# ScalarE copies the turned maxima, and probability tiles and narrow value products are regrouped, in an attention and expert layer

## What is computed

```python
qkv = layernorm(x) @ Wqkv                     # q: 32 heads x 16, k: 16, v: 16
scores = einsum('bqhd,bkd->bhqk', q, k) * scale
scores = where(causal, scores + slopes * (pos_k - pos_q), -1e30)
attn = einsum('bhqk,bkd->bqhd', softmax(scores), v)
x = x + attn @ Wo
y = layernorm(x)
x = x + y @ W_base.T + b_base + expert_delta(y)   # top 2 of 8, rank 16
```

## Time and profile before

| | us |
|---|---|
| median of 3 runs | 700.57 (700.55 to 702.18) |
| the profiled execution | 700.96 |
| its span, first to last instruction | 699.2 |
| TensorE busy in it | 669.7 |
| VectorE busy | 557.4 |
| ScalarE busy | 358.6 |
| GpSimd busy | 216.9 |

### The profile page before, as it was taken

How to read it: one execution, slowest core, us unless ns; L and a number is a source line. 1 busy time by engine, 2 the same in 40 slices (tenths; PEclk the granted TensorE clock), 3 DMA queues, 4 the chain that set the end, 5 groups by cost and what they waited for, 6 DMA issues and landing times.

```text
span 699.2 us, 13261 instructions
## 1 busy us (share of the span) xinstructions
PE 669.7 (96%) x4304; PEld 305.5 (44%) x4304; DVE 557.4 (80%) x1801; ACT 358.6 (51%) x511; POOL 216.9 (31%) x366
## 2 busy tenths in 40 slices
PE   3889999999999999999999999999999999999997
PEld 2434344544344444444443343433433455555553
DVE  5899889887989889898988989899881365666565
ACT  2324647567556676666666666767667411111111
POOL 0035424233332515243352231422432412222220
PEclk9999999999999999999999999999999999999999
DMA  8578108080411443080144744225200189700001
GB/s 253 130 145 137 64 2 136 30 147 28 166 54 51 60 89 108 11 131 34 41 63 94 102 81 77 49 49 94 48 18 33 52 130 170 162 30 30 31 30 60
DMA packets 42951, 56.32 MB, mean 81 GB/s; under 512 B 6648, under 2 KB 26232, under 8 KB 42752
## 3 DMA queue, kind: packets, MB, share of 16 engines
q1 hardware_dynamic: 40296, 51.27, 37.3%
q10 hardware_dynamic: 2592, 4.26, 1.8%
HBM read 35.72 MB, written 19.79 MB: 79 GB/s over the span
## 4 chain that ended last, share of the span: by engine, by line
PE 83%; DVE 10%; DMA 3%; ACT 2%; issue 1%; SPq 1%; POOL 0%; DVEq 0%; ACTq 0%; POOLq 0%
PE psum L780 20%; PE psum L732 18%; PE psum L762 13%; PE psum L808 8%; PE psum L830 7%; PE psum L678 7%; PE psum L759 5%; DVE psum L1145 3%; PE psum L825 2%; PE psum L840 2%; ACT work L965 2%; DMA x_sb<-in_x 1%; DVE negm L1150 1%; PE psum L817 1%; DMA arena<-q_dram 1%
## 5 line engine op out<-in xcount | busy, mean ns | idle before, releaser
L965 ACT ACTIVATE work<-psum 128x1024 f32<-128x1024 f32 (+1 forms) x320 | 289.0, 943 | 127.6 <-PE psum L762 108.5
L1145 DVE CUSTOM_DVE_ANT_0 psum<-psum,future 128x384 f32<-128x384 f32 (+3 forms) x512 | 237.7, 514 | 12.6 <-PE psum L732 10.4
L732 PE MATMUL psum<-k_op,arena 106*128 106x512 bf16 (+3 forms) x768 | 212.4, 328 | 9.6 <-DVE negm L1145 4.3
L1150 DVE TENSOR_REDUCE negm<-psum 128x1 f32<-128x512 f32 x256 | 168.6, 687 | 15.3 <-PE psum L732 10.9
L1318 POOL TENSOR_SCALAR_AFFINE_SELECT work<-work 128x512 f32<-128x512 f32 x128 | 81.2, 634 | 296.2 <-ACT work L965 296.2
L780 PE MATMUL psum<-work,v_op 128*32 128x512 f32 (+3 forms) x1536 | 163.5, 498 | 0.5 <-POOL work L1318 0.4
L762 PE MATMUL psum<-arena,k_op 109*128 109x512 bf16 (+3 forms) x640 | 157.3, 316 | 1.9 <-ACT work L965 0.8
L732 PEld LDWEIGHTS psum<-k_op,arena 106*128 106x128 bf16 x768 | 69.0, 97 | 128.5 <-DVE negm L1145 40.7
L678 PE MATMUL psum<-arena,wqkv_sb 128*128 128x256 f32 (+3 forms) x240 | 84.6, 453 | 1.1 <-ACT arena L887 1.1
L759 PE MATMUL psum<-arena,k_op 116*128 116x128 bf16 x512 | 84.3, 221 | 0.9 <-ACT work L965 0.9
L762 PEld LDWEIGHTS psum<-arena,k_op 109*128 109x128 bf16 x640 | 59.6, 98 | 44.5 <-ACT work L965 15.7
(11 more groups left out here) (86 smaller groups left out, 454.8 us busy)
## 6 DMA issues: line engine op xcount, KB each, us to landing
arena<-q_dram SPq DMA_DIRECT2D x96, 128.0 KB, 5.5
o_dram<-o_sb SPq DMA_DIRECT2D x32, 256.0 KB
q_dram<-arena SPq DMA_DIRECT2D x16, 384.0 KB, 4.4
arena<-o_dram SPq DMA_DIRECT2D x32, 128.0 KB, 4.6
arena<-rcp_dram SPq DMA_DIRECT2D x32, 128.0 KB, 4.9
out<-wqkv_sb ACTq DMA_DIRECT2D x16, 256.0 KB, 2.0
x_sb<-in_x SPq DMA_DIRECT2D x3, 1024.0 KB, 10.0
work<-in_x SPq DMA_DIRECT2D x3, 1024.0 KB, 18.8
```

Source lines behind the costliest of these rows:

```text
L732: last = nc.tensor.matmul(bank[:, a * width:(a + 1) * width], q_op[0:ROW_MAX, bass.ds(col, P)], k_op[0:ROW_MAX, b, k0:k0 + width], start=T ...
L965: nc.scalar.activation(probs[:, n % 4, heads * hp:heads * (hp + 1), 0:w], src, ACT.Exp).then_inc(exp_done, 1)
L1145: last = nc.vector.tensor_tensor_reduce(keys, keys, future[:, CH - width:CH], -1.0, 3e38, ALU.add, ALU.min, negm[:, late, 0, j * QT + t:j ...
L1150: nc.vector.tensor_reduce(dst, psum[:, bank, 0:len(js) * width].rearrange("p (a k) -> p a k", a=len(js)), AX_X, ALU.max, negate=True).then ...
```

## The change

1. The rows of maxima are copied by ScalarE (`copy_maxima`), not by VectorE; the turn isn't a slot any more but an entry of its own in TensorE's order. The early turn stays behind the third late slot; the late turn moves from the step's end to behind the third slot of the next step (`TURN_AFTER = (3, 3)`, `turn_behind`).
2. The minimum of full and diagonal maxima falls away: the late diagonal reductions start from the full maximum, read as a value per partition, where they started from 3e38.
3. For the groups m = 3 to 14 (`wide`) the ring of probability tiles has six places, two of them in `x_sb`, and the value products 1, 2, 3 stand in one block behind tile 5's first score piece, 9, 10, 11 in one block behind tile 1's of the next step. In `pe_order` a block has `PV_FIXED` once.

```diff
-TURN = [EARLY_SLOTS + TURN_AFTER, len(SLOTS) + 1]
-SLOTS.insert(TURN[0], ("turn", 0, None, None))
-SLOTS.insert(TURN[1], ("turn", 1, None, None))
...
+PV_TRIPLES = {2: (0,), 5: (1, 2, 3), 6: (4,), 7: (5,), 8: (6,), 9: (7,), 10: (8,)}
+
+def wide(m):
+    return WIDE_FROM <= m < NK - 1
+
+def values_at(k, n):
+    out = []
+    late = k - 2
+    if 0 <= late < NK and n < LAG:
+        if not wide(late):
+            out.append((late, (n - LAG + NTI,)))
+        elif n == LAG - 1:
+            out.append((late, (9, 10, 11)))
+    m = k - 1
+    if 0 <= m < NK and n >= LAG:
+        if not wide(m):
+            out.append((m, (n - LAG,)))
+        elif n in PV_TRIPLES:
+            out.append((m, PV_TRIPLES[n]))
+    return out
+
+def turn_behind(k, put):
+    if put == EARLY_SLOTS + TURN_AFTER[0]:
+        return [("turn", 2 * k, None)]
+    if put == TURN_AFTER[1] and k:
+        return [("turn", 2 * k - 1, None)]
+    return []
...
-        m, v = (k - 1, n - LAG) if n >= LAG else (k - 2, n - LAG + NTI)
-        if 0 <= m < NK:
-            work.append((UH * (CH - TILES[v][2]) + PV_FIXED, ("values", m, v)))
+        for m, some in values_at(k, n):
+            work.append((sum(UH * (CH - TILES[v][2]) for v in some) + PV_FIXED, ("values", m, some)))
...
+            elif what == "turn":
+                bank = banks.pop(0)
+                turn_at[a] = (bank, last[bank])
+                last[bank] = ("turn", a)
+                banks.append(bank)
...
+def probs_slot(m, n):
+    return n % (6 if wide(m) else 4)
...
+        def probs_of(m, n):
+            r = probs_slot(m, n)
+            return ring[:, r] if r < 4 else x_sb[:, r - 4]
...
+            def turn_maxima(u):
+                bank, before = TURN_BANK[u]
+                bank_free(before)
+                pe.wait_ge(slot_free, NSL * (u // 2) + (NSL if u % 2 else EARLY_SLOTS))
+                nc.tensor.transpose(psum[0:UH * QT, bank, 0:P], negm[:, u % 2, 0, :], ident[:]).then_inc(turn_full, 1)
...
                     pe.wait_ge(slot_free, NSL * NK)
+                    pe.wait_ge(turn_done, NU)
...
+            def copy_maxima(u):
+                act.wait_ge(turn_full, u + 1)
+                if u >= 2:
+                    act.wait_ge(m_split, u - 1)
+                nc.scalar.copy(m_t[:, u % 2], psum[0:UH * QT, TURN_BANK[u][0], 0:P]).then_inc(turn_done, 1)
...
-                    if kind == "turn":
-                        u = 2 * k + late
+                    if k and r in (0, EARLY_SLOTS):
+                        dve.wait_ge(turn_full, 2 * k - 1 + late)
+                    dve.wait_ge(slot_full, idx + 1)
+                    width = P * (t + 1) if kind == "diag" else CH
+                    if kind == "diag":
                         if late:
...
+                            dve.wait_ge(slot_free, NSL * k + SLOTS.index(("full", 1, t, js[-1:])) + 1)
...
+                            last = nc.vector.tensor_tensor_reduce(keys, keys, future[:, CH - width:CH], -1.0,
+                                                                  negm[:, 1, 1, at:at + 1] if late else 3e38, ALU.add, ALU.min,
+                                                                  negm[:, late, 0, at:at + 1])
```

More of the change, by code:

```diff
@@ L168, in vector_time @@
     kind, _, t, _ = SLOTS[r]
[L169 removed]
+    time = 680 if kind == "full" else (550, 750, 500, 700)[t]
     if r in KEY_SLOTS.get(k, ()):
@@ L217, in pe_order @@
         done += w
-        while k < NK and put < NSL - 1 and slot_due(k, put) * total <= done:
+        while k < NK and put < NSL and slot_due(k, put) * total <= done:
             out.append(("slot", k, put))
             put += 1
+            out += turn_behind(k, put)
         out.append(piece)
-    return out + [("slot", k, r) for r in range(put, NSL if k < NK else 0)]
+    for r in range(put, NSL if k < NK else 0):
+        out.append(("slot", k, r))
+        out += turn_behind(k, r + 1)
+    return ([("turn", NU - 1, None)] if k == NK else []) + out
 ORDER = [pe_order(k) for k in range(NK + 2)]
 def places():
-    slot_at, use_at, last = {}, {}, [None] * NSB
+    slot_at, use_at, turn_at, last = {}, {}, {}, [None] * NSB
     for u in range(N_FIRST):
@@ L267, in uses_behind @@
             piece = b
-        if what == "side" and b == len(use_parts(USES[a])) - 1:
-            out.setdefault(piece, []).append(a)
+        if what == "turn" or what == "side" and b == len(use_parts(USES[a])) - 1:
+            out.setdefault(piece, []).append((what, a))
     return out
@@ L983, in step @@
                 behind = uses_behind(k)
-                for u in behind.get(None, ()):
-                    side(u)
+                for piece in behind.get(None, ()):
+                    evict(*piece)
                 for n in range(NTI):
@@ L1117, in _, with step @@
             KEY_PIECES = 7
-            def step(k, i=None, some=range(NSL)):
+            def step(k, some=range(NSL)):
                 for r in some:
```

85 lines of the change are left out of this document (41 added, 44 removed).

## The result

The changed kernel takes **719.5 us** (median of 4 executions, 719.1 to 722.8) against 701.4 of the kernel before in the same session (700.6 to 702.2): a ratio of **1.027**, 95% interval 1.023 to 1.030, slower. The forecast was 714.4 within 703 to 721, slower at 0.85. The side was right and the time lies in the range; the growth is 18.1 us where I had 13.8.

A forecast was written before the change was run, and what follows sets the result against it. TensorE, busy 96% of the span, was taken to set steps 4 to 15. Joints save 12.0 us, but waits on ScalarE and VectorE outweigh them: net +13.8 on 700.57 gives 714.4 us, range 703 to 721.

The forecast's parts named there:

- both leashes: TensorE's limits: three PSUM banks feed VectorE, and only two score pieces may be written ahead of ScalarE.
- The joints: Joining value products in the early and late blocks saves 0.25 us each; 48 joints, 12.0 us less.
- The third score piece: In steps 5 to 15 it waits for ScalarE's first exponential, starting 1.78 after the first piece: 0.62 us a step.
- d7 and d8: Slots ahead of the late block wait for VectorE's banks: 0.55 us, plus 0.34 in steps without projections.
- The early block: Score pieces and slots ahead of it, or the turn, wait on ScalarE and VectorE: 0.9 us a step.
- The late turn: Behind the next step's third slot it waits 0.5 for a bank instead of 0.31: 0.2 us a step, steps 2 to 16.
- VectorE's relief: Copies, minima and idling off VectorE remove small TensorE waits: 0.3 us in steps without projections, 0.1 with.
- The start value: 256 late diagonal reductions read a per-partition start value: 0 to 0.06 us each possible, taken as 0.
- Steps 0 to 4: Steps 0 and 1 gain 1.0 us; steps 2 and 3 lose 0.4, step 4 loses 0.4 for its early block.
- The score wait alone: Rival: slots ahead of the blocks find banks free, leaving score and turn waits; 696 to 701, about 699 us; chance 0.11.
- the full gain: Rival: neither ScalarE's nor VectorE's limit is reached; about 688 us, 685 up to 692; chance 0.05.
- the start value costs: Rival: per-partition start values lengthen VectorE's late reductions, adding 6 us; 718 to 723, about 720; chance 0.12.

The follow-up runs named there:

- e1: Changed kernel without its blocks: every value product single, ring of four; ScalarE's copies, moved turns and start value stay. 706.7 us, 1.005 of the kernel before.
- e2: Kernel before with only the blocks and the ring of six added; VectorE still turns and copies. 720.5 us, 1.025 of the kernel before.
- e5: Changed kernel with early blocks alone; products 9, 10, 11 single again. 713.3 us, 1.016 of the kernel before.
- e6: Changed kernel with late blocks alone; products 1, 2, 3 single again. 714.7 us, 1.018 of the kernel before.
- e10: Changed kernel with the first two exponentials of each unit pair, from step 4 on, over half the columns. 716.8 us, 1.021 of the kernel before.
- e7: Changed kernel with the late turn one slot later, behind the next step's fourth slot. 715.3 us, 1.019 of the kernel before.
- e3: Changed kernel with late diagonal reductions started from the constant again, leaving late full tiles' maxima out of the result. 718.2 us, 1.022 of the kernel before.
- e4: Changed kernel with step 0's early turn alone four slots later in TensorE's order. 722.4 us, 1.029 of the kernel before.
- e12: e8 with VectorE's one reciprocal moved from behind step 10's late turn to between the minimum and the copy. 699.2 us, 0.994 of the kernel before.
- e8: Kernel before, VectorE turning and copying, with early blocks only, in steps 4 to 9 that have query projections. 700.1 us, 0.997 of the kernel before.

## Why the prediction was right, and where its sum was short

- **What bounds, and the direction.** Right. The blocks do save TensorE's time, and more comes back as waits on both leashes. e1, e2, e5, e6 and e10 show it by taking the parts away.
- **The joints.** Taken at 0.25, 1.0 a step. Step 13's length less all its waits, small ones included, fell from 26.8 (0.98 of waits) to 25.9 (3.6): 0.9, or 0.23 a joint. The estimate from the Trainium skill's two pages (TensorEngine Tiling (Array Packing), Key Properties; TensorE: Matmul & The Clock Gate, Single matmul latency), 0.35 a joint, was not borne out.
- **The third score piece.** Taken at 0.62, measured 0.67, 1.78 after the first as walked; and by e10 it is on the path in full.
- **d7 and d8.** 0.55 and 0.34; measured 0.55 and 0.35, and 0.55 alone in step 8.
- **The early block.** 0.9; measured 0.97 in step 13 and, over the three places named, 0.31 + 0.14 + 0.52 in step 8.
- **The late turn.** Mis-sized: a wait of 0.64 instead of 0.5, so 0.33 a step and not 0.2. And a second thing was not seen: that this wait and the third piece's are in a row, so that one slot's distance (e7) takes 0.7 away. The prediction costed the turn's place alone.
- **VectorE's relief.** 0.3 and 0.1 in steps without and with projections; by the small waits 0.23 and 0.12.
- **The step as a whole.** With these terms step 13 closes: -0.92 + 0.33 + 0.67 + 0.90 + 0.97 - 0.23 makes +1.72, where the forecast had +1.3. The mechanism was right, the sizes each a little low; the 29.50 lies just above the 28.7 to 29.3 that I gave as a sign of being right, the 32.29 of step 8 within 31.7 to 32.3.
- **The start value.** The term that failed. I took 0 out of 0 to 0.06 us each, since columns set the pace; it was 0.027 to 0.043, and by e3 3.4 us of the time, of the 4.9 by which the traces' growth of 18.7 lies above my 13.8. In step 13 its 0.23 is contained in the waits above (0.08 of it at f19, the rest in small ones), so it doesn't come on top. Reductions of over 0.71 at 512 columns were one of my signs of being wrong, and they take 0.757. The trace of before had the upper bound, and the middle would have been the better choice. The page I set beside it (the Trainium skill, VectorE: DVE Perf Modes, Two Vector instructions with no wait between them) speaks of the start of the next instruction; what was measured is a longer instruction, so it could not carry the zero.
- **Steps 0 to 4.** Forecast -0.2, measured +1.8. Two things were missing: the early turn's new time, together with the start value (1.1 of it, e3), lets GpSimd run beside VectorE's normalising (+1.6 before step 1), and step 2 is 1.4 longer. e1 has that too and e2 has not, so it comes with the turns: between 112.9 and 123.8 TensorE waits four times for a bank, 1.84 in all, once for ScalarE's copy of a token tile (the row below), three times for VectorE. I had costed ScalarE's copies as hidden without walking the three banks through these steps, in which ScalarE empties some of them. Step 1 is 0.8 shorter: the wait of 0.8 for the maxima's DMA is gone (see e4). Step 4 is 0.9 shorter where I had it 0.4 longer. I overlooked that product 9 moves out of it into step 5's block, so that step 4 has four 384-column matmuls less than before; an isolated one of these products takes 0.79. In the steps between one product comes in for each that leaves.

```profile
113.58 0.39 PE L794 MATMUL psum<-k_op,arena 106*128 106x512 bf16 x1 [0.37 <-ACT arena L961]
```

- **Step 11.** Not in the sum at all: the reciprocal that cost 1.65 in the kernel before costs 0.3 in after. By e12 it is the reciprocal; that it is cheap in after because VectorE no longer waits there for the turn is argued, not tested. Without this gain the kernel would have been some 20 us slower.
- **The sum by stretches** of the profiled executions: steps 0 to 4 +1.8 (forecast -0.2), 5 to 9 +7.3 (+6.0), 10 to 15 +9.1 (+7.8), the rest +0.5 (+0.4): +18.7.
- **The rivals.** The score wait alone and the full gain are refuted by the same rows; "the start value costs" had the right mechanism at 6 us where 3.4 was measured. The sum that I wrote under the score wait alone gives 696.0, the low end of its range and not its centre of 699.

## What to carry to other kernels

Before work of one engine is joined in a block, ask what it was doing between the pieces: products between score pieces and slots were the time in which ScalarE and VectorE freed their banks, and a joint's 0.23 us was paid for with waits of 0.35 to 0.67. The only block that gained here had other work (projections) between its slots, and VectorE's turns (e8); with ScalarE's turns it cost 0.29 in the same steps. A forecast must walk each bank from its release to its next use, and look at the first and last steps by themselves, where a product that moves is not replaced. And an instruction that is placed once, like a reciprocal of 1.7 us, is worth looking for: moved into an idle stretch it brought 1.5 us, nearly as much as e8's six blocks together (1.9).

## What the runs showed of the hardware

- After TensorE had been busy for 0.68 and then 1.57 of two 2-us stretches, its granted clock was 0.50 for 6.8 us (e2, step 11). In the same place it stayed at 1.00 with waits of 0.78, 0.51 and 0.40 (after), and with one of 1.32 behind which TensorE was busy throughout (before: 0.69, then 2.00 of two 2-us stretches).
- VectorE's SBUF-to-SBUF TENSOR_SCALAR of 128x512 took 0.73 to 1.52 us beside GpSimd's work instead of 0.54 (after, e4). The slowest was 2.8 times its usual time. Not every overlap costs VectorE: in e3 one of the four took 0.54 while GpSimd's TENSOR_TENSOR beside it took 1.38 instead of 1.15. By the Trainium skill, GPSIMD Engine Reference, Specifications, the SBUF interfaces of the two engines are shared, with contention for VectorE's instructions in a 2-port mode or with two SBUF inputs. The trace agrees that the two engines slow each other; whether this instruction is of those kinds, no run shows.
- A reduction with a start value per partition takes 27 to 43 ns more than with a constant (after, 128 to 512 columns).
